# Two copies exchanged on ScalarE and a split moved to the head of its step on VectorE, in a fused two-layer kernel

## The reference

```python
# L0_cond: x scaled by the condition, multiplied by a weight, and scaled per sequence and feature
# L0_attn, 16 heads of 64:
qkv = inputs @ W_qkv
q, k, v = jnp.split(qkv, 3, axis=-1)
score = jnp.einsum('bihd,bjhd->bijh', q, k) / D ** 0.5
masked_score = score * mask + 1e+30 * (mask - 1.0)
wmat = jax.nn.softmax(masked_score, axis=2)
out = jnp.einsum('bijh,bjhd->bihd', wmat, v).reshape(b, l, H * D)
return out @ W_out          # and x = x + this
# L0_cond2, on the new x: three projections, then a scan over the tokens
forget_gate = jax.nn.sigmoid(input_seq @ W_f.T + b_f)
input_gate = jax.nn.sigmoid(input_seq @ W_i.T + b_i)
candidate = input_seq @ W_h.T + b_h
```

## Time and profile before

| | us |
|---|---|
| three runs | 1025.86, 1024.60, 1023.19 |
| median | 1024.6 |
| profiled execution | 1025.86 |
| its span in the profile | 1024.6 |
| PE busy | 976.7 (95%) |
| DVE busy | 878.3 (86%) |
| ACT busy | 831.3 (81%) |
| POOL busy | 468.6 (46%) |

### The profile page before, as it was taken

The page is one execution under the profiler, slowest core; times in us unless marked ns, Lnnn a source line. Parts: engine busy times, 40 slices in busy tenths (PEclk is TensorE's granted clock), DMA queues, the critical chain, the costliest instruction groups (busy, mean ns, idle before and its releaser), DMA issues.

```text
span 1024.6 us, 25937 instructions
## 1 busy us (share of the span) xinstructions
PE 976.7 (95%) x8929; PEld 787.0 (77%) x8929; DVE 878.3 (86%) x3720; ACT 831.3 (81%) x2230; POOL 468.6 (46%) x539
## 2 busy tenths in 40 slices
PE   5999999999999999999979999999899999999897
PEld 5899898888888989743258988888777777776566
DVE  5777989898989898799998899898988888896985
ACT  4888888888888888887787877876778888886786
POOL 1334545454545463606900102101878888893041
PEclk9999999999999999999999999999999999999899
DMA  9000000000000000000000000000000000000002
GB/s 404 2 3 2 2 2 2 2 2 2 2 2 2 2 2 2 2 1 0 1 1 1 1 1 1 1 11 11 23 23 23 22 24 23 23 3 1 1 2 83
DMA packets 8579, 18.31 MB, mean 18 GB/s; under 512 B 1280, under 2 KB 5504, under 8 KB 8064
## 3 DMA queue, kind: packets, MB, share of 16 engines
q1 hardware_dynamic: 8448, 16.65, 4.8%
HBM read 10.36 MB, written 2.10 MB: 12 GB/s over the span
## 4 chain that ended last, share of the span: by engine, by line
PE 78%; DVE 9%; ACT 7%; POOL 3%; issue 2%; DMA 1%; SPq 0%; DVEq 0%; ACTq 0%; POOLq 0%
PE PB L243 8%; PE PB L244 8%; PE PB L245 8%; PE PB L338 6%; PE PB L393 6%; PE PB L376 6%; PE PB L1790 5%; PE PB L1190 3%; PE PB L1192 3%; PE PB L1191 3%; PE PB L1762 3%; PE PB L1807 3%; PE PB L425 2%; PE PB L426 1%; PE PB L427 1%
## 5 line engine op out<-in xcount | busy, mean ns | idle before, releaser
L368 POOL TENSOR_TENSOR W<-W,small 128x512 f32<-128x512 f32 x128 | 138.4, 1082 | 220.8 <-DVE small L362 220.8
L357 ACT ACTIVATE W<-W,small 128x128 f32<-128x128 f32 x512 | 198.8, 391 | 28.8 <-DVE small L348 28.1
L243 PE MATMUL PB<-RR_s 128*128 128x256 f32 (+3 forms) x568 | 184.9, 326 | 5.9 <-DVE RR_s L1142 2.5
L244 PE MATMUL PB<-RR_s 128*128 128x256 f32 (+3 forms) x568 | 177.1, 312 | 0.0
L245 PE MATMUL PB<-RR_s 128*128 128x256 f32 (+3 forms) x568 | 177.0, 312 | 0.0
L348 DVE CUSTOM_DVE_ANT_0 W<-PB,W 128x128 f32<-128x128 f32 x512 | 117.3, 284 | 39.5 <-PE PB L338 38.5
L1778 POOL TENSOR_TENSOR AR_s<-AR_s,small 128x512 f32<-128x512 f32 x128 | 129.4, 1040 | 29.2 <-DVE small L1771 29.1
L1164 ACT ACTIVATE AR_s<-PB,W 128x512 f32<-128x512 f32 (+2 forms) x160 | 100.5, 629 | 29.7 <-PE PB L245 23.2
L243 PEld LDWEIGHTS PB<-RR_s 128*128 128x128 f32 x568 | 108.9, 192 | 14.3 <-issue 4.7
L1178 DVE TENSOR_TENSOR RR_s<-AR_s,RR_s 128x512 fp32r<-128x512 f32 (+2 forms) x160 | 99.8, 633 | 17.4 <-ACT RR_s L1169 13.7
L1771 DVE CUSTOM_DVE_ANT_0 AR_s<-PB,W 128x128 f32<-128x128 f32 x512 | 111.0, 286 | 2.7 <-PE PB L1762 0.5
(11 more groups left out here) (380 smaller groups left out, 2434.2 us busy)
## 6 DMA issues: line engine op xcount, KB each, us to landing
W<-in_w SPq DMA_DIRECT2D x1, 5809.5 KB, 23.9
XF<-in_xT SPq DMA_DIRECT2D x4, 512.0 KB, 9.2
out<-XT SPq DMA_DIRECT2D x8, 256.0 KB, 2.3
W<-in_w SPq DMA_DIRECT2D x1, 1088.0 KB, 5.3
W<-in_w SPq DMA_DIRECT2D x1, 1024.0 KB, 8.1
W<-AR_s SPq DMA_DIRECT2D x16, 64.0 KB, 2.1
AR_s<-AR_s SPq DMA_DIRECT2D x16, 64.0 KB, 2.1
QS<-AR_s SPq DMA_DIRECT2D x12, 64.0 KB, 2.1
```

The costliest lines, as they stand in the source:

```text
L243: nc.tensor.matmul(out, lh, rh, start=True, stop=False)
L244: nc.tensor.matmul(out, ll, rh, start=False, stop=False)
L357: e = nc.scalar.activation(SS[r][:, hl], SS[r][:, hl], ACTF.Exp, bias=mx[r][:, h:h + 1], scale=-1.0, accum_out=rc[r][:, h:h + 1])
L368: nc.gpsimd.tensor_tensor(s3, s3, over(rc[r], 2, [128, 4, 128]), ALU.mult).then_inc(s_nrm, 1)
```

## The change

On ACT, in every step, the copy of the second transposes `act_pt(2v-1)` now comes ahead of the copy of v, `act_vp(v+1)`. On DVE, the half-0 split `dve_xl(c, 0)` moves from near the end of step v = 8c+7 to its head, where the half-1 splits already stand. Eight instructions move on DVE, 63 pairs are exchanged on ACT; nothing is added or removed, and PE's and POOL's lists are the same.

```diff
--- before.py
+++ after.py
@@ -679,10 +679,10 @@
                     act_exp(2 * v + 1)
                 if v % 4 == 1 and v // 4 + 1 < NCH:
                     act_uh(v // 4 + 1)
+                if 0 <= v - 1 < NV:
+                    act_pt(2 * v - 1)
                 if v + 1 < NV:
                     act_vp(v + 1)
-                if 0 <= v - 1 < NV:
-                    act_pt(2 * v - 1)
                 if v in (1, 2):
                     act_wout(v - 1)
                 if v == 4:
@@ -711,9 +711,8 @@
             dve_qk(2)
             dve_qk(3)
             for v in range(NV + 1):
-                for c, hf in split_steps(v):
-                    if hf:
-                        dve_xl(c, hf)
+                for s in split_steps(v):
+                    dve_xl(*s)
                 if v < NV:
                     dve_max(2 * v)
                 if 0 <= v - 3 < NV:
@@ -732,9 +731,6 @@
                     dve_gated(*step)
                 if v < NV:
                     dve_rc(2 * v + 1)
-                for c, hf in split_steps(v):
-                    if not hf:
-                        dve_xl(c, hf)
                 for step in dve_gate_steps(2 * v + 1):
                     dve_gated(*step)
                 if v % 4 == 1 and v // 4 + 1 < NCH:
```

## The result

The change made the kernel slower: 1032.6 us (median of 6 runs, 1030.74 to 1033.55) beside 1025.2 for the kernel before (6 runs, 1023.15 to 1026.09, the three known ahead of the prediction among them). The ratio is 1.0075, with a 95% interval from 1.0059 to 1.0089. The forecast was 1022.7 with a range to 1026.4: wrong, in size and in sign.

The account below looks back on a forecast made before the run. PE, busy 95% of the span, was taken as the bound, with waits for ACT in six steps. From 1025.86 us, -1.92 + 0 + 0 + 0 gave 1023.9, or 1022.7 from the median; range 1020.6 to 1026.4.

Parts of the forecast that it names:

- Old place: Steps v = 16 to 56 behind a moved split: PE's wait for ACT goes, 7.05 to 6.73 us, 6 x 0.32 = 1.92 us.
- New place: Head of steps like 47: the split issues at 321.67, goes ahead of POOL's L557, and maxima start as before; cost 0.
- The reading of the lock: DVE and POOL: issue order decides who blocks; DVE goes first even when issuing only 0.06 us ahead of POOL.
- Rival (a): POOL goes first at the new place, maxima 1.11 us late, PE waits at T(93): +3.8 us net, 1028.4; chance 12%.
- Exchange: Copies on ACT: v copy 0.5 us later, next bank user the k matmuls with 0.89 us of room; 0 both directions.
- The end: Step 63, end of the stage: what the chain loses in the split it pays at the lock; 0, ends -0.6 and +0.8.

Follow-up runs that it names:

- experiment 4: Kernel before with only the half-0 split moved and its wait for the gate projections put a step earlier, on L505: 1024.9 us, ratio 1.0003.
- experiment 8: Kernel before with only the half-0 split moved and the two waits ahead of it in swapped order: 1023.0 us, ratio 0.9985.
- experiment 2: Kernel before with only the half-0 split moved to the head of its step, old copy order on ACT: 1028.4 us, ratio 1.0039.
- Experiment 1: Kernel before with only the two copies on ACT exchanged, splits at their old place: 1029.0 us, ratio 1.0044.
- experiment 5: Kernel before with only the copies on ACT exchanged, except in steps 8c+3 and 8c+4, which keep the old order: 1024.5 us, ratio 0.9998.
- experiment 9: Kernel before with half-0 splits moved and their two waits swapped, but the last group's first half at its old place: 1022.9 us, ratio 0.9985.
- experiment 7: Kernel before with the half-0 split put right behind the second maxima of step 8c+7, where POOL runs nothing: 1023.0 us, ratio 0.9980.
- experiment 3: The whole change with the half-0 split's wait for the gate projections put a step earlier, on L505: 1026.1 us, ratio 1.0016.
- experiment 6: As experiment 4, but the last group's first half taken from the head of step 63 to behind the gate scans L522: 1024.7 us, ratio 0.9998.

## Why the prediction was wrong, point by point

- **Old place, 6 x 0.32.** Right. Six steps 8c went from 7.05 to 6.73 us (-1.96 to -2.01 in every kernel with the split gone from there).
- **New place, "Cost 0".** This is the step that failed, +5.2 us where the sum has 0. It put DVE's issue at 321.67, 0.02 us behind L451, "by the example of step 51". That example is the half-1 split, with one wait; the moved one has two, and started 0.10 us behind, too late to be ahead of L557. Experiments 4 and 8 show it from both sides: with the wait for L451 carried by the split the start is 0.03 us behind and the step costs nothing; with that wait on an instruction ahead of the split, 0.87 us a step. The reading of the lock held: who starts first goes first, by 0.05 us one way (experiment 4) and by 0.02 the other (the change). The Trainium skill (SBUF — State Buffer, "Who interferes with whom") says that issue order decides who blocks; both traces agree.
- **Rival (a), 12%.** Its mechanism is what happened, and its margin, "a delay of L451 by 0.06 us", was right in size; the delay came on DVE. Its sizes: maxima 1.09 us late (1.11 forecast), a step 0.87 us longer (0.96). It had all of PE's wait at T(93). Most of it lay earlier, at the v projection that waits for L405, 0.58 us against 0.21. Given a margin of some hundredths, 12% was far too low: nothing in the rows measured it for an instruction with two waits. That its time, 1028.4, is also the median of experiment 2 is luck in part: the loop there is 3.26 us longer, not 3.8, and the rest lies outside the loop.
- **Exchange, "Both directions: 0".** The second failed step, +2.4 us. The bank's next user was taken to be the k matmuls of the next step, in every step. In the steps 8c+3 the order k, k, v, gate, gate, PV makes PV of the same step the next user. The room there was 0.12 us, not 0.89. The table of waits that rows 2 come from held the sign already: in the kernel before, PE's weight loads for PV (L393) are released by L323 seven times, 2.6 us in all. The rule of the banks stood in the kernel's own text (`pe_drained`, three places before); it was applied to one kind of step only. Experiment 1 shows the loss and that it is only there; with the old order in these steps and the steps 8c+4 (experiment 5) it is gone.
- **The end, 0 between -0.6 and +0.8.** It was +0.15 (experiment 8 against 9). The 0.33 us by which the maxima were to be late came true (1.21 us behind the scores in the changed kernel, 0.88 before); the scans, which were to lose at POOL's L562 what the split gives, start 6.21 us behind the scores instead of 5.99.
- **What was in no step.** +0.3 us ahead of the first scores, and +0.85 in the later stages, mostly from two more stretches at the lower clock. Both differ from trace to trace without a tie to the edit: the first scores by 1.4 us over all traces here, the stretches as the last section shows.

In sum: -1.9 forecast and -2.0 found; +5.2 and +2.4 in the two terms that were set to zero.

## What to carry to other kernels

A move that relies on starting just ahead of another engine's instruction needs the start of that very instruction with its own waits; a twin with one wait less is no measure. Where there are two waits, write them so that the one that comes last is carried by the instruction itself (here that was the one written first, experiments 2 and 8), or, safer, choose a place where the other engine is idle (experiment 7). And when a copy is put later, list the next user of its bank for every kind of step, since one added use in some steps turns the round.

## What the runs showed of the hardware

- **A second wait costs about 0.07 us of start when it is the late one.** Split behind the end of L451: 0.10 us with the late wait on the instruction ahead (the change and experiment 2), 0.03 us with it on the split (4 and 8), in each of the six steps 8c+7. In that order the already satisfied wait costs nothing that shows.
- **The lock between VectorE and POOL turns on hundredths.** Split ahead of L557 by 0.05 us: 0.42 us long. Behind it by 0.02: 1.54 us. The loser of a turn goes before the winner's next instruction (L558 stretched to 1.49 us).
- **TensorE's granted clock falls for short stretches in the later stages, in some traces and not in others, and what each costs differs.** In 30 us windows from 455, 515 and 710 us the changed kernel has a granted clock of 0.94 in all three, which is 3.4 us at the lower level, 1.2 GHz instead of 2.4, in each (0.50 from 472.1 to 475.3, for one); the kernel before only in the first, and experiments 3, 7, 8 and 9 in none:

```profile
455.00:485.00 30.00, 28.01 (x79) 9.60 (x77) 28.58 (x61) 22.12 (x42) 12.60 (x12) 0.94 0.00 0
515.00:545.00 30.00, 24.82 (x98) 16.37 (x96) 28.39 (x69) 25.36 (x42) 3.05 (x3) 0.94 0.00 1
710.00:740.00 30.00, 28.34 (x257) 23.70 (x255) 27.08 (x125) 21.58 (x38) 13.98 (x19) 0.94 0.07 17
```

  The columns are the window, its length, busy time of PE, PEld, DVE, ACT and POOL, granted clock, DMA share and GB/s. PE is busy for 25 to 28 of the 30 us in them, and as much in the same windows without a fall. Set beside experiment 8, the first costs 1.65 us, the second 0.3, the third 0.4; together that is more than the gain sought. Of the 35 runs of the kernel before beside experiments 5 to 8, the six with a mean granted clock of 0.996 or more take 1023.1 to 1023.6 us and the eight with 0.995 take 1025.8 to 1026.5. These runs have no traces of their own, so that the stretches explain the spread is likely but not shown. What sets them off was not tried.
- **Open: 0.35 us in steps 17 and 49** of experiments 3, 4 and 6, all with the wait moved to L505. VectorE's first maxima start that much late though the scores' semaphore is met, with no releaser in the trace. No DMA fetch of instructions holds the maxima up by its recorded time: in step 49 none starts in the 4 us ahead of them. What differs is when one queue fetches: in the kernels without the loss 0.2 to 0.5 us behind the scores of step 17 and 2.0 to 2.3 us ahead of those of step 49, in these three only 0.9 to 1.2 and 1.85 us behind them. Whether that belongs to the cause wasn't tested.
